# Cross attentions of a two-layer decoder: GpSimd's order of routed rows, norm power and projection bias

## The chip, the cores and the metric

The kernel runs on one core of a Trainium2 chip. The metric is the device time of one execution in microseconds (us), lower is better. Five engines work side by side and meet only at semaphores: TensorE (PE, matrix products; PEld is its weight load), VectorE (DVE), ScalarE (ACT), GpSimd (POOL) and SyncE (SP). DMAs are issued from the queues of SP and POOL and run on the core's 16 DMA engines.

## The reference

Eight sequences of 256 tokens with 256 features go through two layers. In both, a self-attention, a cross-attention to 77 context rows and a mixture of eight experts (the two best are taken for every token) add to the tokens `x`:

```
x = x + _L0_attn_ref(_layernorm(x, axis=-1), ...)
x = x + _L0_xattn_ref(_layernorm(x, axis=-1), ctx_1024, ctx_1024, ...)
x = x + _L0_ffn_ref(_layernorm(x, axis=-1), ...)       # top 2 of 8 experts
x = x + _L1_attn_ref(_layernorm(x, axis=-1), ...)
x = x + _L1_xattn_ref(ctx_1024, ctx_1024, _layernorm(x, axis=-1), ...)
x = x + _L1_ffn_ref(_layernorm(x, axis=-1), ...)       # top 2 of 8 experts
```

A cross-attention's output projection has a bias (`bo`), and the norm that follows it feeds the router of the experts.

## The kernel before

The change lies in `attention_crossed`, which runs once in each layer (names begin with L0x and L1x). It works through B = 8 batches (sequences) of 256 tokens. A batch is two tiles of 128 tokens (QT_N = 2) and is worked on in two units u = 2b + c, one for each half of the heads. The order of the work is written out by hand, once for every engine, as a loop over the units; no scheduler moves anything. Several batches are in flight in one turn of the loop. While the attention of batch b runs:

- the first norm (before the attention) is made for batch b+2: DVE statistics, POOL `spread_norm`, ACT `norm`;
- batch b-1 gets its projection added (DVE `add`, L498) and then its second norm, the one for the router: DVE statistics (L501 to L506), POOL `route_norm` (four small instructions, L255 to L258: add epsilon, the power -1/2, the product with the mean, the sign), ACT `route_norm` (L627, which writes the normed rows `xr`), PE transposes of `xr` (L804) and the router's product (L809);
- batch b-2 gets its two experts chosen (DVE `choose`, L514 to L529), and batch b-3 its slots in the experts' table (DVE `slots`, up to L546);
- `send` (L744) scatters the rows of batch b-3 into the table `expert_table` in device memory: an indirect DMA on POOL's queue for each of the two tiles and each of its two experts, four for a batch, each of 128 rows of 260 floats. Each adds 16 to the semaphore `scattered[b % 2]`.

The rows to be sent stand in `xr[b % 2]`, two buffers. So ACT's `route_norm` of batch b, which overwrites the buffer of batch b-2, has to wait until all of batch b-2's rows have been scattered:

```
eng.wait_ge(r_rstd_done, b + 1)
if b >= 2:
    eng.wait_ge(scattered[par], b // 2 * 64)
```

The bias of the projection is added to X by POOL (`bias`, L725) ahead of DVE's `add` of the same batch, which comes two units later. SP's queue waits for scattered rows at three places: it loads early blocks of the table (L2167) when batches 0 to 3, and then 0 to 4, have been sent, and the rest at the end. POOL's `send` of batch 4, and of batch 5, in turn waits for these early loads to land (`early_landed`), in front of its first tile. Behind the loop POOL sends batch 5, adds to the experts' part, and works on the second norm and the rows of batches 6 and 7.

On PE the order in a unit with c = 0 is: the scores of the next unit, the transposes of maxima, the query projection (L300), the transposes of `xr` (L804), the values of the unit before (L865), the turned scores (L850).

Of the kernel before, what the change touches and what calls it, by code (L numbers as in the profile page):

```python
# [309 lines left out]
def attention_crossed(nc, name, env, wo, bo, first, route, experts, final):  # L310
# [33 lines left out]
    with ExitStack() as stack:  # L344
# [95 lines left out]
        with nc.Block(no_gpsimd_drain=True) as block:  # L440
            @block.sync
            def _(eng):
                for b in range(B):
                    eng.wait_ge(added, b + 1)
                    tiles = slice(b * QT_N, (b + 1) * QT_N)
                    eng.dma_start(route["sums"].rearrange("(t p) d -> p t d", p=P)[:, tiles, :], X[:, tiles, :]).then_inc(route["kept"], 16)
                    if b == ORDER_BY + 1:
                        experts["first_loads"](eng)
                    for i, last in enumerate(FULL_BY):
                        if b == last + 1:  # L450
                            for par in range(2):
                                eng.wait_ge(scattered[par], ((last - par) // 2 + 1) * 64)
                            experts["load_early"](eng, i)
                for sc in scattered:
                    eng.wait_ge(sc, B // 2 * 64)
                experts["sync"](eng)
# [260 lines left out]
            @block.gpsimd  # L717
            def _(eng):
                def route_norm(b):
                    first["spread"](eng, b, r_mv, r_veps, r_rstd, r_offset, r_shift_by, r_var_done, r_rstd_done)  # L720

                def bias(b):
                    xb = X[:, b * QT_N:(b + 1) * QT_N, :]
                    eng.wait_ge(xn_done, b + 1)
                    eng.tensor_tensor(xb, xb, bo[:, :].unsqueeze(1).to_broadcast([P, QT_N, D]), ALU.add).then_inc(biased, 1)  # L725

                def odds_of(b):

                    eng.wait_ge(apart_done, b + 1)
                    eng.wait_ge(slot_done, b)  # L730
                    eng.tensor_tensor(odds[:, :], env["e"][:, 0:QT_N], apart[:, :], ALU.pow).then_inc(odds_done, 1)

                def send(b, tiles=range(QT_N)):
                    par = b % 2
                    eng.wait_ge(slot_done, b + 1)
                    if b == 0:
                        for s, v in route["zeroed"]:
                            eng.wait_ge(s, v)
                    for i, last in enumerate(FULL_BY):
                        if b == last + 1 and tiles[0] == 0:  # L740
                            eng.wait_ge(*experts["early_landed"][i])
                    for q in tiles:
                        for k in range(TOP):
                            eng.indirect_dma_start(route["table"], bass.IndirectOffsetOnAxis(ap=slot_i[:, par, q, k:k + 1], axis=0),  # L744
                                                   xr[:, par, q, :], None).then_inc(scattered[par], 16)

                for i in range(2):
                    eng.memset(tops[i][:, :, :], 0.0).then_inc(cleared, 1)
                first["clear"](eng, 1)
                first["weights_in"](eng)  # L750
                if ("b", 0) in events:
                    eng.wait_ge(first["bias_out"], 1)
                for u in range(units):
                    b, c = part(u)
                    if c == 0:
                        if b + 2 < B:
                            first["spread_norm"](eng, b + 2)
                        if b >= 3:
                            send(b - 3)
                    else:  # L760
                        bias(b)
                        if b >= 1:
                            route_norm(b - 1)
                x = experts["pool_parts"](eng)
                send(B - 3)
                x["start"]()
                odds_of(B - 2)
                route_norm(B - 1)
                x["add"](0)
                send(B - 2, [0])  # L770
                odds_of(B - 1)
                send(B - 2, [1])
                send(B - 1)
                for n in range(1, len(EARLY)):
                    x["add"](n)
                x["rest"]()
# [1968 lines left out]
```

## Time and profile before

| | us |
|---|---|
| median of 3 runs | 1502.38 |
| lowest and highest | 1500.22, 1503.75 |
| the profiled execution, device time | 1504.03 |
| its span in the trace | 1502.4 |
| cross-attention of layer 0 in the trace | about 225 to 385 |
| cross-attention of layer 1 in the trace | about 1078 to 1240 |
| TensorE busy, mean of the span | 95% |

The profiled execution lies 1.65 us over the median, and its span leaves out 1.6 us around the program. A time worked out in the trace is added to 1504.03; against the median it reads 1.65 us less. Both cross-attentions have the same structure, so a row of one layer stands for both unless said otherwise.

### The profile page before, as it was taken

What the parts mean: (1) busy time and instruction counts of PE and PEld (TensorE: products, weight loads), DVE (VectorE), ACT (ScalarE), POOL (GpSimd) and SP (SyncE); (2) the same over time, 40 slices, a digit from 0 to 9 for tenths busy, and PEclk for the clock granted to TensorE, in tenths of its full rate; (3) what the DMA queues carried; (4) which work ended last, traced back from release to release, by engine and by line L of the source; (5) the groups of instructions that cost most, each with busy time, mean ns of one, the idle gap of its engine ahead of it and who ended that gap; (6) DMA issues with size and microseconds to landing.
All of it is one profiled execution on the core that took longest, in us unless ns stands there. A gap on an engine that the chain in (4) does not pass through costs nothing. (4 is left out here: it accounts for less than half of the span.)

```text
span 1502.4 us, 34667 instructions
## 1 busy us (share of the span) xinstructions
PE 1433.9 (95%) x11880; PEld 1159.7 (77%) x11881; DVE 748.7 (50%) x2160; ACT 619.1 (41%) x1711; POOL 490.5 (33%) x758
## 2 busy tenths in 40 slices
PE   7999998988999999999999999999899899999998
PEld 5676766767899999976777777777666579999997
DVE  6666757887433333344444444444278862222222
ACT  2433346653222222235445444545366533333332
POOL 3545442444322122223233233333224452222222
PEclk9999999999999999999999999999999999999999
DMA  9920000152243434120000000000001522533332
GB/s 316 333 69 2 2 2 9 45 176 62 50 119 67 144 71 114 32 64 1 0 1 1 1 1 1 1 1 0 1 16 44 174 78 40 149 93 94 94 90 34
DMA packets 79666, 97.46 MB, mean 65 GB/s; under 512 B 10523, under 2 KB 72579, under 8 KB 79555
## 3 DMA queue, kind: packets, MB, share of 16 engines
q1 hardware_dynamic: 64643, 77.58, 16.4%
q0 software_dynamic: 13680, 17.19, 6.6%
q8 instruction: 73, 1.20, 0.3%
q10 hardware_dynamic: 1232, 1.18, 0.2%
q14 instruction: 38, 0.31, 0.1%
HBM read 57.51 MB, written 39.59 MB: 65 GB/s over the span
## 5 line engine op out<-in xcount | busy, mean ns | idle before, releaser
L1741 POOL TENSOR_TENSOR L1a_prob<-L1a_prob,L1a_rtot 128x1024 f32<-128x1024 f32 x64 | 121.1, 1892 | 275.8 <-DVE L1a_rtot L1614 275.8
L2270 PEld LDWEIGHTS L0x_ps<-L0f_rows_t,L0f_w_up 128*128 128x128 f32 x1584 | 183.7, 193 | 10.4 <-issue 9.0
L2270 PE MATMUL L0x_ps<-L0f_rows_t,L0f_w_up 128*128 128x128 f32 x1584 | 185.8, 277 | 5.6 <-issue 4.8
L2346 ACT ACTIVATE L1f_hid<-L1x_ps,L1f_b_up 128x128 f32<-128x128 f32 x296 | 92.4, 363 | 163.0 <-PE L1x_ps L2270 159.7
L2270 PEld LDWEIGHTS L1x_ps<-L1f_rows_t,L1f_w_up 128*128 128x128 f32 x1184 | 139.5, 194 | 3.4 <-issue 1.6
L2270 PE MATMUL L1x_ps<-L1f_rows_t,L1f_w_up 128*128 128x128 f32 x1184 | 140.4, 277 | 0.6 <-ACT L1f_rows_t L2330 0.6
L2279 PE MATMUL L1x_ps<-L1f_w_down,L1f_hid 128*128 128x256 f32 x592 | 134.1, 380 | 1.9 <-issue 1.9
L2214 POOL TENSOR_TENSOR turn<-eps 128x1 f32<-128x1 f32 x74 | 13.6, 184 | 372.3 <-DVE wv L2448 367.7
L1683 ACT ACTIVATE L1a_prob<-L1a_ps_s,L1a_nmax 128x256 f32<-128x256 f32 x256 | 118.2, 473 | 38.1 <-DVE L1a_nmax L1609 38.1
L2279 PEld LDWEIGHTS L1x_ps<-L1f_w_down,L1f_hid 128*128 128x128 f32 x592 | 109.6, 190 | 15.5 <-issue 2.1
L1245 POOL TENSOR_SCALAR_AFFINE_SELECT L0a_prob<-L0a_prob 128x128 f32<-128x128 f32 (+1 forms) x256 | 79.8, 353 | 104.3 <-ACT L0a_prob L1199 104.3
L2338 ACT ACTIVATE ctx_in<-L0x_ps 128x256 f32<-128x256 f32 x72 | 27.6, 383 | 183.1 <-PE L0x_ps L2270 157.1
L2279 PE MATMUL L0x_ps<-L0f_w_down,L0f_hid 128*128 128x256 f32 x432 | 99.4, 380 | 1.7 <-DVE L0f_hid L2435 1.7
L1199 ACT ACTIVATE L0a_prob<-L0a_ps 128x384 f32<-128x384 f32 x128 | 52.4, 497 | 108.0 <-PE L0a_ps L1331 108.0
L1609 DVE TENSOR_REDUCE L1a_nmax<-L1a_ps_s 128x2 f32<-128x512 f32 x128 | 79.2, 681 | 31.4 <-PE L1a_ps_s L1805 31.4
L2279 PEld LDWEIGHTS L0x_ps<-L0f_w_down,L0f_hid 128*128 128x128 f32 x432 | 79.3, 190 | 11.2 <-DVE L0f_hid L2435 1.9
L1819 PEld LDWEIGHTS L1a_ps_t<-ident,L1a_prob 128*128 128x128 f32 x500 | 59.6, 141 | 34.6 <-issue 26.3
L2435 DVE TENSOR_TENSOR L0f_hid<-ctx_in,L0x_ps 128x256 f32<-128x256 f32 x72 | 30.2, 420 | 106.0 <-ACT ctx_in L2338 70.1
L1819 PE MATMUL L1a_ps_t<-ident,L1a_prob 128*128 128x128 f32 x500 | 76.9, 276 | 3.3 <-DVE L1a_prob_t L1618 2.4
L1618 DVE COPY L1a_prob_t<-L1a_ps_t 128x512 f32<-128x512 f32 x63 | 42.8, 680 | 58.3 <-PE L1a_ps_t L1819 58.3
L1693 ACT ACTIVATE L1a_prob_t<-L1a_ps_t 128x512 f32<-128x512 f32 x62 | 37.1, 598 | 81.5 <-PE L1a_ps_t L1819 81.5
L2425 DVE TENSOR_SCALAR token<-L1f_from_end 128x1 int32<-128x1 f32 x37 | 5.7, 153 | 126.8 <-DMA out_dram<-wv,token 126.8
(486 smaller groups left out, 2812.5 us busy)
## 6 DMA issues: line engine op xcount, KB each, us to landing
expert_table<-zero SPq DMA_DIRECT2D x1, 16640.0 KB, 68.5
L0f_w_up<-in_w_dram SPq DMA_DIRECT2D x8, 1408.0 KB, 6.8
L1f_w_up<-in_w_dram SPq DMA_DIRECT2D x8, 1024.0 KB
L1f_w_down<-in_w_dram SPq DMA_DIRECT2D x8, 1024.0 KB
L0f_w_down<-in_w_dram SPq DMA_DIRECT2D x8, 768.0 KB, 8.7
L1f_rows<-expert_table SPq DMA_DIRECT2D x35, 130.0 KB
L0f_rows<-expert_table SPq DMA_DIRECT2D x32, 130.0 KB
sums<-X SPq DMA_DIRECT2D x8, 256.0 KB
```

Of the source, the lines that this page charges most:

```text
L1199: eng.activation(prob[u % 2][:, r, :, :], bank("p", u, r)[:, 0:KT * W].rearrange("p (t w) -> p t w", t=KT), ACT.Exp).then_inc(exp_done, 1)
L1245: ins = eng.affine_select(out=p, in_=p, compare_op=ALU.is_ge, fill=0.0, base=base, pattern=[[0, 2], [sign, n]], channel_multiplier=-sign)
L1609: eng.tensor_reduce(nmax[:, j % RING, :], src, AX.X, ALU.max, negate=True).then_inc(max_done, 1)
L1618: eng.tensor_copy(prob_t[s % 2][:, k, :], turn_bank(b, s, k)).then_inc(even_out, 1)
L1683: ins = eng.activation(prob[:, j % RING, q, :], ps_s[:, k, q * S:(q + 1) * S], ACT.Exp, bias=nmax[:, j % RING, q:q + 1], accum_out=total[: ...
L1693: eng.activation(prob_t[s % 2][:, k, :], turn_bank(b, s, k), ACT.Copy).then_inc(odd_out, 1)
L1741: eng.tensor_tensor(v, v, r.unsqueeze(2).to_broadcast([P, 2 * QT_N, S]), ALU.mult).then_inc(norm_done, 1)
L1819: ins = eng.transpose(out[:, o:o + P], prob[:, j % RING, q, c * P:(c + 1) * P], ident[:, :])
L2270: ins = eng.matmul(ps_h[c][:, o:o + P], w_up[par][:, t, w0:w0 + P], rows_t[:, t, :], start=(t == 0), stop=(t == DT - 1))
L2279: ins = eng.matmul(ps_y[:, 0:D], hid[:, c, k * P:(k + 1) * P], w_down[par][:, 2 * c + k, :], start=(c == 0 and k == 0), stop=(c == CHUNKS ...
L2346: ins = eng.activation(hid[:, c, k * P:(k + 1) * P], ps_h[c][:, k * P:(k + 1) * P], ACT.Gelu, bias=b_up[par][:, 2 * c + k:2 * c + k + 1])
L2435: ins = eng.tensor_tensor(hid[:, c, :], mid[:, c, :], ps_h[c][:, 2 * P:4 * P], ALU.mult)
```

## The change

POOL's loop over units is reordered. Before, the unit c = 0 issued `spread_norm(b + 2)` and all four scatters of batch b-3, and the unit c = 1 the bias of batch b and then the second norm of batch b-1. Now the unit c = 0 scatters only tile 0 of batch b-3 (two DMAs); the unit c = 1 first does the second norm of batch b-1, then scatters tile 1 of batch b-3 (two DMAs), and adds the bias of batch b last. No instruction is added or taken away, and no other engine's order is touched.

```diff
                         if b >= 3:
-                            send(b - 3)
+                            send(b - 3, [0])
                     else:
-                        bias(b)
                         if b >= 1:
                             route_norm(b - 1)
+                        if b >= 3:
+                            send(b - 3, [1])
+                        bias(b)
```

POOL in the cross-attention of layer 0, batch b = 3, the first with a `send`. Before:

```order
L744 DMA expert_table<-L0x_xr,L0x_slot_i 17024x260 [waits zeroed,L0x_slot_done]
L744 DMA expert_table<-L0x_xr,L0x_slot_i 17024x260 x3
L725 TENSOR_TENSOR X<-X,bo 128x512 [waits L0x_xn]
L255 TENSOR_TENSOR L0x_r_veps<-L0x_r_mv,eps 128x2 [waits L0x_r_var]
L256 TENSOR_TENSOR L0x_r_rstd<-L0x_r_veps,neg_half 128x2 [waits L0x_link_g]
L257 TENSOR_TENSOR L0x_r_offset<-L0x_r_mv,L0x_r_rstd 128x2 [waits L0x_link_g]
L258 TENSOR_SCALAR L0x_r_shift_by<-L0x_r_offset 128x2 [waits L0x_link_g]
L255 TENSOR_TENSOR L0x_veps<-L0x_mv,eps 128x2 [waits L0x_var]
```

and of the change at the same place:

```order
L744 DMA expert_table<-L0x_xr,L0x_slot_i 17024x260 [waits zeroed,L0x_slot_done]
L744 DMA expert_table<-L0x_xr,L0x_slot_i 17024x260
L255 TENSOR_TENSOR L0x_r_veps<-L0x_r_mv,eps 128x2 [waits L0x_r_var]
L256 TENSOR_TENSOR L0x_r_rstd<-L0x_r_veps,neg_half 128x2 [waits L0x_link_g]
L257 TENSOR_TENSOR L0x_r_offset<-L0x_r_mv,L0x_r_rstd 128x2 [waits L0x_link_g]
L258 TENSOR_SCALAR L0x_r_shift_by<-L0x_r_offset 128x2 [waits L0x_link_g]
L744 DMA expert_table<-L0x_xr,L0x_slot_i 17024x260 [waits zeroed,L0x_slot_done]
L744 DMA expert_table<-L0x_xr,L0x_slot_i 17024x260
L725 TENSOR_TENSOR X<-X,bo 128x512 [waits L0x_xn]
L255 TENSOR_TENSOR L0x_veps<-L0x_mv,eps 128x2 [waits L0x_var]
```

Two of the four DMAs and the bias have moved behind the second norm, which itself waits for DVE's statistics (`r_var`).

ACT at the same place, which is the same before and after (the second norm of batch 2, L627, and what follows it):

```order
L660 ACTIVATE L0x_counts<-L0x_ps 128x32 [waits L0x_made]
L627 ACTIVATE L0x_xr<-X,L0x_r_shift_by,L0x_r_rstd 128x256 [waits L0x_scattered0,L0x_r_rstd]
L627 ACTIVATE L0x_xr<-X,L0x_r_shift_by,L0x_r_rstd 128x256
L232 ACTIVATE L0x_q_raw<-L0x_ps,bq1s 128x256 [waits L0x_made]
L232 ACTIVATE L0x_q_raw<-L0x_ps,bq1s 128x256
L236 ACTIVATE L0x_q_m<-L0x_q_raw,L0x_none,half_mask 128x2x256 [waits L0x_q_out]
```

Nothing moved on ACT; `scattered0`, for which L627 waits, is counted up by the four DMAs of batch 0, two of which stand elsewhere on POOL now.

## Rows read from the trace of the kernel before

**Rows 1.** The page: busy us of each engine, share of the span, instructions.

```profile
PE 1433.9 (95%) x11880; PEld 1159.7 (77%) x11881; DVE 748.7 (50%) x2160; ACT 619.1 (41%) x1711; POOL 490.5 (33%) x758
```

**Rows 2.** Busy time by window, five batches, layer 0: length, busy us by engine, clock.

```profile
276.20:292.70 16.50, 15.93 (x178) 11.39 (x171) 13.77 (x37) 11.38 (x26) 6.96 (x10) 1.00 0.14 50
292.70:308.40 15.70, 15.45 (x184) 10.87 (x180) 15.12 (x44) 9.93 (x23) 8.13 (x15) 1.00 0.16 53
308.40:326.20 17.80, 15.43 (x180) 10.82 (x176) 16.33 (x62) 10.09 (x22) 7.68 (x12) 1.00 0.74 262
326.20:342.80 16.60, 13.40 (x172) 9.01 (x168) 13.00 (x41) 7.31 (x17) 6.55 (x9) 1.00 0.31 102
342.80:359.00 16.20, 13.75 (x144) 10.19 (x141) 14.30 (x45) 7.20 (x15) 8.12 (x11) 0.89 0.24 74
```

**Rows 3.** Timeline of POOL, batch 3, layer 0: start, length, instruction, idle before, releaser.

```profile
277.10 1.22 POOL L744 DMA_INDIRECT expert_table<-L0x_xr,L0x_slot_i  x1 [0.66 <-issue]
...
281.18 0.96 POOL L744 DMA_INDIRECT expert_table<-L0x_xr,L0x_slot_i  x1 [0.30 <-issue]
282.17 1.27 POOL L725 TENSOR_TENSOR X<-X,bo 128x512 f32<-128x512 f32 x1
286.68 0.19 POOL L255 TENSOR_TENSOR L0x_r_veps<-L0x_r_mv,eps 128x2 f32<-128x2 f32 x1 [3.24 <-DVE L0x_r_mv L506]
...
288.04 0.22 POOL L258 TENSOR_SCALAR L0x_r_shift_by<-L0x_r_offset 128x2 f32<-128x2 f32 x1
292.74 0.20 POOL L255 TENSOR_TENSOR L0x_veps<-L0x_mv,eps 128x2 f32<-128x2 f32 x1 [4.48 <-DVE L0x_mv L183]
```

**Rows 4.** Timeline of ACT and PE behind POOL's norm, batch 3, layer 0.

```profile
287.36 1.89 PE L300 MATMUL L0x_ps<-L0x_xt,wq 128*128 128x256 f32 x8
...
288.30 1.09 ACT L627 ACTIVATE L0x_xr<-X,L0x_r_shift_by,L0x_r_rstd 128x256 f32<-128x256 f32 x2 [1.79 <-POOL L0x_r_shift_by L258]
...
289.53 0.63 PE L804 MATMUL L0x_ps<-ident,L0x_xr 128*128 128x128 f32 x4 [0.28 <-ACT L0x_xr L627]
```

**Rows 5.** Timeline, batch 6, layer 0: last scatter of batch 3, SP's load behind it.

```profile
330.42 0.96 POOL L744 DMA_INDIRECT expert_table<-L0x_xr,L0x_slot_i  x1 [0.30 <-issue]
...
332.23 1.44 DVE L468 TENSOR_REDUCE L0x_tops<-L0x_ps 128x16 f32<-128x1232 f32 x1 [3.05 <-remote]
...
333.70 0.89 SPq L2167 DMA_DIRECT2D ctx_in<-expert_table  x2
```

**Rows 6.** Timeline, batch 5, layer 1: scatter of batch 2, ACT's wait for it.

```profile
1170.62 0.96 POOL L744 DMA_INDIRECT expert_table<-L1x_xr,L1x_slot_i  x1 [0.30 <-issue]
...
1177.89 1.09 ACT L627 ACTIVATE L1x_xr<-X,L1x_r_shift_by,L1x_r_rstd 128x256 f32<-128x256 f32 x2 [1.14 <-DMA expert_table<-L1x_xr,L1x_slot_i]
```

**Rows 7.** Timeline of PE, layer 1: the projection behind batch 4's second norm.

```profile
1170.66 1.97 PE L797 MATMUL L1x_ps<-wo,L1x_o_t 128*128 128x256 f32 x8 [0.85 <-DVE L1x_o_t L483]
```

**Rows 8.** Timeline of DVE in `choose`, layer 0: batches 3, 4 (with POOL's bias), 7.

```profile
284.12 0.17 DVE L522 CAST L0x_index_f<-L0x_index 128x4 f32<-128x4 uint32 x1
...
298.93 1.78 DVE L522 CAST L0x_index_f<-L0x_index 128x4 f32<-128x4 uint32 x1
...
299.40 1.27 POOL L725 TENSOR_TENSOR X<-X,bo 128x512 f32<-128x512 f32 x1
...
347.65 2.00 DVE L524 TENSOR_TENSOR L0x_chosen<-numbers,L0x_index_f 128x16 f32<-128x16 f32 x2
```

**Rows 9.** Timeline behind the loop, layer 0: second norms of batches 6 and 7.

```profile
356.71 1.09 ACT L627 ACTIVATE L0x_xr<-X,L0x_r_shift_by,L0x_r_rstd 128x256 f32<-128x256 f32 x2 [3.70 <-POOL L0x_r_shift_by L258]
...
360.63 0.60 PE L804 MATMUL L0x_ps<-ident,L0x_xr 128*128 128x128 f32 x4
...
367.14 0.19 POOL L255 TENSOR_TENSOR L0x_r_veps<-L0x_r_mv,eps 128x2 f32<-128x2 f32 x1 [2.07 <-DVE L0x_r_mv L506]
```

**Rows 10.** Busy time by window around the end of layer 0's cross-attention, as rows 2.

```profile
352.00:354.00 2.00, 0.54 (x12) 0.45 (x16) 1.93 (x4) 1.00 (x3) 0.00 (x0) 1.00 0.32 85
...
356.00:358.00 2.00, 2.00 (x12) 2.00 (x11) 1.90 (x7) 1.09 (x2) 1.34 (x4) 0.50 0.04 8
```

## The prediction, made before the change was run

> **What bounds the kernel now.** I read the page first: PE is busy for 95% of the span, POOL for 33% [rows 1]. POOL alone sets nothing, so the change can only act through those who wait for POOL. Then the busy time by window, batch by batch, of layer 0's cross-attention [rows 2]. A batch (two units) takes 15.7 to 17.8 us. In batches 3 and 4 PE is busy for all but 0.6 and 0.3 us, in the later ones for all but 2.4 to 3.2 us; DVE is idle for 2.7, 0.6, 1.5, 3.6 and 1.9 us. So both are near their bound, and a stop of PE that is longer than this idle time has nowhere to hide. Third the timeline of POOL [rows 3]: in batch 3 the four scatters run from 277.10 to 282.14, the bias to 283.44, and then POOL stands idle for 3.24 us until DVE's statistics come; the second norm ends at 288.26. ACT starts its part at 288.30, 0.04 us later [rows 4], and ends at 289.39. PE has just ended the query projection (287.36 + 1.89 = 289.25) and has waited 0.28 us for ACT when its transposes start at 289.53 [rows 4]. So the chain DVE statistics, POOL norm, ACT norm, PE transposes is tight: what delays ACT's L627 delays PE one to one.
>
> **The change, part by part.** The work on POOL stays the same: four scatters, one bias of 1.27 us, four small instructions for each norm. Three things move.
>
> *The bias goes last.* DVE's add needs it two units later, about one batch of 16 us; it now ends some 4 us behind the norm. Between the second norm and the next first norm POOL idled 4.48 us [rows 3], and two scatters and the bias (2.5 + 1.3 us) fit in. I cost it at nothing; without this cover it would be 1.3 us a batch.
>
> It also takes something away. In batch 3 DVE's small conversion L522 takes 0.17 us, in batch 4 1.78 us, and in batch 7 the two L524 together 2.00 us instead of 0.26 [rows 8]. In both slow cases POOL's bias runs at that moment: the 1.78 us end at 300.71, the bias at 300.67 [rows 8]. There are three such places in both layers together (a second CAST of 1.78 us in layer 1), 1.61 + 1.74 + 1.61 = 5.0 us of DVE time at most. With the bias behind the norm they should go. But they lie where PE is the tighter one for most of it, or inside a batch that will now be stopped anyway, so I take 2 us of the 5 as gain (bounds 0 and 5).
>
> *The second norm goes ahead of the bias.* Before, POOL had idled 3.24 us in front of it and waited for DVE each time, so this brings nothing: 0.
>
> *Tile 1's scatters go behind the second norm of batch b-1.* Here the change costs. ACT's L627 of batch b-1 waits for `scattered` of batch b-3, since it overwrites that buffer, and it needs the count of all four DMAs. Two of these are now issued only after POOL has finished the very norm that L627 also waits for. The wait was over by then in nearly all batches; now it always ends last. Its price: 0.2 us to the first issue, 1.06 + 0.30 + 0.96 us for two scatters (the last of the four [rows 3] takes 0.96 us behind 0.30 us of issue; the first one takes 1.22 in batch 3 and 1.06 in the later ones), 2.5 us in sum, and then the landing. For the landing there are two rows. With few other DMAs running, the last scatter of batch 3 ends its issue at 331.38 and SP, which waits for it, issues its load at 333.70 [rows 5]: 2.3 us, an upper bound of the quiet case. While the experts' weights are loaded, the last scatter ends its issue at 1171.58 and ACT, waiting for it, starts at 1177.89 [rows 6]: 6.3 us. So ACT's L627 comes 2.5 + 2.2 = 4.7 us later in a quiet batch, and 2.5 + 6.3 = 8.8 us in batch 5, when those loads run. Behind it on ACT stand the query's outputs, the router's outputs and the exponentials; PE waits at L804, directly behind, with the values (L865) and the turned scores (L850) queued.
>
> Batch by batch, for one layer:
> - b = 3: 4.7, since PE waits for ACT already [rows 4].
> - b = 4: 4.7 less the 0.85 us that PE later waits for DVE [rows 7]: 3.8.
> - b = 5: 8.8 at most. In the next unit DVE now waits 3.05 us for something that the profile only calls remote, right behind the heavy loads [rows 5]; with a stop in front of it I expect that wait to be gone. In layer 0 the loads end sooner behind the scatters. I take 5.0 (bounds 3 and 8.8).
> - b = 6: 4.7.
> - b = 7: ACT's norm of batch 6 ended at 357.80, and PE wants it at 360.63 [rows 9]: 2.8 us of slack, so 4.7 - 2.8 = 1.9.
> - behind the loop: the send of batch 5 waits for the early load, which waits for tile 1 of batch 4. 2.5 us of issue, 2.2 us of landing and a load of 2 to 3 us follow POOL's norm of batch 6 (356.67), so batch 5's four scatters start near 365 instead of 357.17, take 5.1 us, and the norm of batch 7, which waited for DVE until 367.14 [rows 9], starts near 371.5 where the shift by 1.9 alone would give 369. That is about 2.0 for PE (bounds 0 and 3).
>
> Sum of a layer: 4.7 + 3.8 + 5.0 + 4.7 + 1.9 + 2.0 = 22.1 us, for two layers 44.2.
>
> *The clock of TensorE.* At the end of layer 0's cross-attention PE was busy for 0.54 of 2.00 us, and in the window from 356 to 358 the granted clock stood at 0.50 [rows 10], that is 1.2 instead of 2.4 GHz. A stop of 4.7 us is longer, so I expect dips in several of the eight stops of the loop. What of a dip lies in the stop itself costs nothing; 2 us of it behind the stop cost 1 us of work. I take half of that for each stop (bounds 0 and 3), 4 us in all.
>
> Total: 44.2 - 2 + 4 = 46.2. On the profiled execution's 1504.03 this gives 1550.2, against the median 1548.6. I forecast 1550.
>
> **The rivals.**
>
> *A, the clock falls at every stop and stays down.* For it: the dip behind a much shorter gap [rows 10]; against it: only what falls behind the stop costs anything. If each of the eight stops is followed by 3 us lost instead of 0.5, it is 8 x 2.5 = 20 us more: 1570. The Trainium skill's page "TensorE: Matmul & The Clock Gate", Part 1, says that the array's clock goes down to half when PE has been little busy and returns after it has been busy again; by that rule every stop is a candidate, and the trace agrees as far as rows 10 show one.
>
> *B, half of each stop is swallowed.* DVE is the tighter engine in batches 4 and 5 (idle 0.6 and 1.5 us [rows 2]), and while PE stands, DVE can run ahead with statistics and slots. Against it: DVE's next reciprocal needs the values that PE has queued behind L804. If half of the 44 us goes so: 1504 + 22 - 2 = 1524, up to 1530 with dips.
>
> *C, faster.* DVE is the true bound, the stop of 4.7 us falls wholly in time in which PE and ACT would have waited for DVE, and what remains is the 5.0 us of DVE time that the moved bias gives back: 1504 - 5 = 1499. It decides from the point where ACT and PE have 4.7 us of slack at L627. The rows give 0.28 us of wait on the wrong side in batch 3 [rows 4], 0.85 us in batch 4 [rows 7]. The Trainium skill's page "SBUF — State Buffer", section "SBUF: two separate sides", has the rule behind this gain: VectorE and GpSimd share a pair of ports, and an instruction of the one can block the other's for its whole length. The 1.78 us agree with that.
>
> *D, no difference.* The scatters of tile 1 land early enough because POOL comes to them before it waits for `r_var`. The order on POOL excludes it, unless I misread which count L627 waits for: 1504.
>
> **How the numbers follow.** The forecast (1534 to 1566 with its own bounds: 3 to 8.8 for b = 5, 0 to 3 behind the loop, 1 us either way for the landing in each stop) gets 0.72, A 0.12, B 0.10, C 0.03, D 0.03. The range from 1524 to 1572 takes in A and most of B. A measurement of this kernel can tell about 0.2%, 3 us, from no change. So slower has 0.72 + 0.12 + 0.10 = 0.94, the same 0.03, faster 0.03.
>
> **What would show it.** In the profile of the changed kernel: L627 waiting for the DMA of `expert_table` in ten places (batches 2 to 6 of both layers), 4 to 5 us behind POOL's L258, up to 9 us in batch 5; PE idle in front of L804 for the same time; batches of 20 to 22 us in both cross-attentions; L522 back at 0.17 us; the experts and self-attentions unchanged. It would be wrong if L627 still waited for POOL's L258, or if PE's idle time in front of L804 were well under 4 us. Shorter dips or none would take 4 us off; a landing nearer to 1 us than to 2.2 would take off some 10.

## The result, and the profile after

| | before | after |
|---|---|---|
| median of 3 runs, us | 1502.38 | 1568.46 |
| lowest and highest, us | 1500.22, 1503.75 | 1566.29, 1571.29 |
| span of the profiled execution, us | 1502.4 | 1566.8 |
| mean granted clock of TensorE in it | 0.993 | 0.965 |

The change makes the kernel slower: the ratio is 1.0444, 95% interval 1.0418 to 1.047, or 66 us. That lies in the predicted range (1524 to 1572), but 18 us over the forecast of 1550, and close to the 1570 of rival A. One execution behind this document, of the kernel with only the bias moved, took 2110.34 us at a mean clock of 0.651; the ratios leave it out.

First the page of the kernel after, its engines' busy us and shares, to be held against [rows 1]:

```profile
PE 1472.6 (94%) x11880; PEld 1185.8 (76%) x11881; DVE 744.6 (48%) x2160; ACT 618.4 (39%) x1711; POOL 490.9 (31%) x758
```

The instruction counts are the same. PE is busy for 38.7 us more (1472.6 against 1433.9) with exactly the same products, and idle for 25.7 us more (1566.8 - 1472.6 = 94.2 against 1502.4 - 1433.9 = 68.5). These two add up to the 64.4 us by which the span grew. So waiting is the smaller part of the loss; the larger is that PE works more slowly.

Next where it lies, in two windows of each kernel that begin and end at the same events (length, busy us of PE, PEld, DVE, ACT and POOL, clock, DMA share, GB/s): first from the end of layer 0's experts over layer 1's self-attention to the start of its cross-attention, then the experts of layer 0. Before, then after:

```profile
640.60:1078.20 437.60, 428.79 (x2587) 319.99 (x2585) 197.16 (x417) 211.56 (x677) 134.29 (x93) 1.00 0.02 6
396.00:640.60 244.60, 239.01 (x1789) 227.06 (x1788) 82.47 (x334) 52.15 (x153) 53.74 (x62) 1.00 0.36 87
```

```profile
668.20:1105.70 437.50, 428.77 (x2587) 320.32 (x2585) 197.35 (x417) 211.53 (x677) 134.26 (x92) 1.00 0.02 6
423.50:668.20 244.70, 239.04 (x1789) 227.17 (x1788) 82.51 (x334) 52.16 (x153) 53.75 (x62) 1.00 0.36 87
```

Both stretches are unchanged to 0.1 us. All of the loss is in the cross-attentions with their tails (from the clearing of `tops` to the first transposes of the experts' rows): 170.7 to 198.3 us in layer 0, 172.5 to 209.7 in layer 1, or 27.6 and 37.2 us.

Now the view of one line, for ACT's L627: what it waited for, and who waited for it (PE's transposes of `xr` stand at L806 now), us and times. Before it had waited 1.1 us once for a DMA.

```profile
  DMA expert_table<-L1x_xr,L1x_slot_i: 30.0, 5
  DMA expert_table<-L0x_xr,L0x_slot_i: 26.4, 5
...
who waited for it (us, times):
  PE L1x_ps L806: 20.9, 5
  PE L0x_ps L806: 18.0, 6
```

Five waits in each layer, ten in all, as the prediction listed. In the timeline of batch 3, layer 0, the chain of [rows 3, 4] reads now:

```profile
287.26 1.89 PE L300 MATMUL L0x_ps<-L0x_xt,wq 128*128 128x256 f32 x8
...
287.94 0.22 POOL L258 TENSOR_SCALAR L0x_r_shift_by<-L0x_r_offset 128x2 f32<-128x2 f32 x1
...
288.66 1.06 POOL L744 DMA_INDIRECT expert_table<-L0x_xr,L0x_slot_i  x1 [0.50 <-issue]
...
290.02 0.97 POOL L744 DMA_INDIRECT expert_table<-L0x_xr,L0x_slot_i  x1 [0.30 <-issue]
291.02 1.27 POOL L725 TENSOR_TENSOR X<-X,bo 128x512 f32<-128x512 f32 x1
292.56 1.09 ACT L627 ACTIVATE L0x_xr<-X,L0x_r_shift_by,L0x_r_rstd 128x256 f32<-128x256 f32 x2 [6.16 <-DMA expert_table<-L0x_xr,L0x_slot_i]
```

```profile
293.80 0.95 PE L806 MATMUL L0x_ps<-ident,L0x_xr 128*128 128x128 f32 x4 [4.65 <-ACT L0x_xr L627]
```

POOL's norm ends at 288.16, as before. Then come the two scatters, the second of which ends its issue at 290.99; 1.57 us later ACT starts, 4.40 us behind the norm where it had been 0.04. PE has waited 4.65 us in place of 0.28, and its four transposes then take 0.95 us instead of 0.63. The last number leads to the clock. Windows of the kernel after in which the granted clock stands at half (columns as in [rows 2]); four of layer 0, then four of layer 1:

```profile
294.00:297.40 3.40, 3.40 (x25) 2.19 (x26) 1.55 (x6) 3.08 (x7) 0.00 (x0) 0.50 0.00 0
314.50:324.70 10.20, 10.20 (x78) 6.41 (x75) 6.66 (x22) 5.00 (x10) 2.33 (x4) 0.50 0.63 202
338.40:348.60 10.20, 10.20 (x72) 6.75 (x63) 5.04 (x13) 3.56 (x9) 0.36 (x1) 0.50 0.05 15
358.90:365.70 6.80, 6.59 (x53) 3.06 (x53) 2.69 (x8) 0.66 (x2) 1.94 (x2) 0.50 0.37 119
...
1178.10:1191.70 13.60, 13.46 (x89) 9.00 (x90) 7.79 (x27) 6.41 (x13) 3.40 (x6) 0.50 0.06 21
1222.50:1236.10 13.60, 11.97 (x84) 7.72 (x85) 4.39 (x7) 5.68 (x11) 0.22 (x1) 0.50 0.08 30
1246.40:1260.00 13.60, 12.34 (x72) 7.96 (x72) 5.35 (x24) 4.00 (x9) 1.94 (x2) 0.50 0.18 60
1273.70:1283.90 10.20, 9.53 (x37) 8.74 (x38) 1.49 (x13) 3.58 (x12) 5.26 (x7) 0.50 0.36 119
```

The delayed L806 start at 293.80, 313.81, 337.00 and 359.11 in layer 0; the windows begin from 0.2 us ahead of them to 1.4 us behind. In layer 1 they begin 0.1 to 1.7 us ahead of L806, while PE still stands. So in these eight places the clock goes down (from 2.4 to 1.2 GHz) when PE has just gone on or is about to, and the half speed falls almost wholly on the work behind the stop: PE is busy for 88% of such a window or more. Behind the two shortest waits of the ten, those of L806 at 1202.27 (1.83 us) and 382.96 (1.44 us), no such window begins. Over the span, but for one at its very end in both kernels, there are 13 such stretches with 105.8 us, of which PE is busy for 100.9; before there were 3 with 17.1 us, busy for 16.3. That is 100.9 - 16.3 = 84.6 us more of work at half speed. At full speed it would take half as long, so 42 us of it would be stretch, against the 38.7 us that PE is busier.

### The profile page after: what moved, and what is told of

It is laid out like the page before. It is cut to its first block and busy times, and to the rows that moved or that the text cites. A ratio compares the mean times of both kernels' runs of the same rounds, so it can differ in the third digit from the quotient of the medians.

```text
span 1566.8 us, 34669 instructions
## 1 busy us (share of the span) xinstructions
PE 1472.6 (94%) x11880; PEld 1185.8 (76%) x11881; DVE 744.6 (48%) x2160; ACT 618.4 (39%) x1711; POOL 490.9 (31%) x758
## 5 line engine op out<-in xcount | busy, mean ns | idle before, releaser
L2272 PEld LDWEIGHTS L0x_ps<-L0f_rows_t,L0f_w_up 128*128 128x128 f32 x1584 | 185.7, 195 | 10.6 <-issue 9.2
L2272 PE MATMUL L0x_ps<-L0f_rows_t,L0f_w_up 128*128 128x128 f32 x1584 | 188.1, 279 | 5.7 <-issue 4.8
L2272 PEld LDWEIGHTS L1x_ps<-L1f_rows_t,L1f_w_up 128*128 128x128 f32 x1184 | 140.8, 195 | 3.4 <-issue 1.6
L2272 PE MATMUL L1x_ps<-L1f_rows_t,L1f_w_up 128*128 128x128 f32 x1184 | 141.7, 279 | 0.6 <-ACT L1f_rows_t L2332 0.6
L2216 POOL TENSOR_TENSOR turn<-eps 128x1 f32<-128x1 f32 x74 | 13.6, 184 | 374.4 <-DVE wv L2450 370.7
L1110 DVE TENSOR_REDUCE L0a_tops<-L0a_ps 128x2 f32<-128x384 f32 x128 | 62.5, 552 | 12.1 <-PE L0a_ps L1316 12.1
```

Of the source, the lines that this page charges most:

```text
L1110: eng.tensor_reduce(tops[u % UNITS][:, :, at_row], src, AX.X, ALU.max, negate=True).then_inc(max_done, 1)
L2272: ins = eng.matmul(ps_h[c][:, o:o + P], w_up[par][:, t, w0:w0 + P], rows_t[:, t, :], start=(t == 0), stop=(t == DT - 1))
```

## The experiments

The median of the kernel before was 1500.1 to 1500.5 us in all of these; ratios are against it. The change itself was timed beside 1502.38, so differences between its 1568.46 and the medians below can be off by some 2 us. The theory at the outset: the loss is the late landing of tile 1's rows, which ACT waits for in ten places, with PE stopping directly behind it, and some part of it is TensorE's clock. Rivals: the moved bias; the scatters being issued in two parts; a loss by stops alone.

### Which of the moved steps costs

The bias alone goes last, all four scatters stay ahead of the norm:

```diff
                             send(b - 3)
                     else:
-                        bias(b)
                         if b >= 1:
                             route_norm(b - 1)
+                        bias(b)
```

> Only the bias moves: all four scatters stay in the unit c = 0, the second norm comes next, the bias last. Theory (the loss is ACT's L627 waiting for tile 1's scatters): nothing of the loss is here, and the three places where DVE's L522 or L524 took 1.6 to 1.7 us longer beside the bias go: 1497 to 1502 us, no L627 waiting for the DMA beyond the 1.1 us of the kernel before. Rival (the late bias delays DVE's add or the next first norm): over 1510, with DVE's L498 waiting for POOL.

Measured: 1500.33 us, ratio 0.9993 (0.9982 to 1.0004). Tile 1's scatters alone go behind the norm, the bias stays where it was:

```diff
-                            send(b - 3)
+                            send(b - 3, [0])
                     else:
                         bias(b)
                         if b >= 1:
                             route_norm(b - 1)
+                        if b >= 3:
+                            send(b - 3, [1])
```

> Only tile 1's scatters move behind the second norm; the bias stays ahead of the norm. Theory: the whole loss of 66 us is here, 1560 to 1572 us, with L627 waiting for the DMA in ten places, 4.1 to 5 us behind L258 and about 8 us once in layer 1. Rival (half of the loss is the bias's): 1530 to 1545.

Measured: 1567.33 us, ratio 1.045 (1.0428 to 1.0472). And the scatters in two parts, but tile 1's ahead of the norm, with the bias last:

```diff
-                            send(b - 3)
+                            send(b - 3, [0])
                     else:
-                        bias(b)
+                        if b >= 3:
+                            send(b - 3, [1])
                         if b >= 1:
                             route_norm(b - 1)
+                        bias(b)
```

> The scatters are split as in the change, but tile 1's stand ahead of the second norm: unit c = 1 is scatter, norm, bias. Theory (what costs is that the scatter is queued behind a norm that waits for DVE, not the split): POOL issues tile 1 directly behind tile 0, so 1497 to 1503 us. Rival (the split or its additional waits cost by themselves): over 1510.

Measured: 1500.14 us, ratio 0.9995 (0.9985 to 1.0006). So the whole loss belongs to one thing, the place of tile 1's scatters behind the norm. Cutting the send in two costs nothing, and moving the bias neither costs nor gains in these kernels. In the kernel with only the bias moved, the view of the line L522 (duration in ns: min, median, max) shows that the conversions of 1.78 us [rows 8] are gone:

```profile
L522 DVE CAST L0x_index_f<-L0x_index x8: 170/170/421, 265.6 to 373.6; 128x4 f32<-128x4 uint32 x8
L522 DVE CAST L1x_index_f<-L1x_index x8: 170/170/415, 1122.9 to 1225.8; 128x4 f32<-128x4 uint32 x8
```

The time that DVE got back did not reach the end.

### The wait for the buffer

A third pair of buffers for `xr` and `slot_i` in layer 0, on top of the change: L627 of batch b then waits for the rows of batch b-3, sent a batch ago. Layer 1 stays as in the change.

```diff
-        xr, xr_t = sb("xr", [P, 2, QT_N, ROW]), sb("xr_t", [P, DT, S])
+        XB = 2 if final else 3
+        xr, xr_t = sb("xr", [P, XB, QT_N, ROW]), sb("xr_t", [P, DT, S])
...
-                    if b >= 2:
-                        eng.wait_ge(scattered[par], b // 2 * 64)
+                    if b >= XB:
+                        eng.wait_ge(scattered[b % XB], b // XB * 64)
```

> The changed order in full, but in layer 0 alone the routed rows and their slots have three buffers, so ACT's L627 waits for the scatters of three batches earlier; layer 1 keeps two. Theory: layer 0 loses nothing any more in the loop and little behind it (the sends of batch 5 still wait for the early load), its share of about half of the 66 us goes: 1532 to 1542 us, L0x_xr with no wait for the DMA, no TensorE clock dips in layer 0's loop, and layer 1 as in the changed kernel. Rival (the late scatters themselves, through SP's loads or the DMA queue, cost): layer 0 keeps over 10 us of its loss, over 1545.

Measured: 1544.8 us, ratio 1.0294 (1.0274 to 1.0315). The line L628 (L627 with one line more ahead of it): what it waited for, and who waited for it (PE's transposes of `xr` stand at L807):

```profile
  DMA expert_table<-L1x_xr,L1x_slot_i: 28.9, 5
...
  PE L1x_ps L807: 20.4, 6
  PE L0x_ps L807: 5.2, 3
```

The wait for the DMA is gone in layer 0 and is there in layer 1. Layer 0's stage takes 176.0 us (170.7 before, 198.3 in the change), layer 1's 207.7 (209.7 in the change). POOL's order is that of the change in both. So what costs is the wait for the buffer, not the order on POOL as such: 22.3 of layer 0's 27.6 us go with it. What remains, 5.3 us, is in the tail, where batch 5 is still sent late: at batch 6's transposes this kernel stands at 360.66 and the kernel before at 360.63, at batch 7's it stands at 373.93 against 369.99, with PE waiting for the late norm:

```profile
373.93 0.63 PE L807 MATMUL L0x_ps<-ident,L0x_xr 128*128 128x128 f32 x4 [4.11 <-ACT L0x_xr L628]
```

My expectation left that too small, which is why it was missed by 3 us. It also missed on the clock: one half-clock stretch of 3.4 us stands inside layer 0's loop (from 344.4), where the change had four. A third buffer in the kernel before was not run; there L627 had waited for the DMA only once, 1.1 us in layer 1.

### One and four scatters behind the norm

Three scatters ahead of the norm and one behind it, and in the second kernel none ahead and four behind:

```diff
-                            send(b - 3, [0])
+                            send(b - 3, [0], [(0, 0), (0, 1), (1, 0)])
...
-                            send(b - 3, [1])
+                            send(b - 3, [1], [(1, 1)])
```

> Dose, downward: of batch b-3's four scatters three stay ahead of the second norm and only the last one stands behind it. Theory (each stop is the issue behind the norm plus the landing of about 1.6 us): L627 comes 2.9 to 3.2 us behind L258 instead of 4.1 to 4.5, so 1.27 us less in ten places, and fewer or shorter half-clock stretches: 1540 to 1556 us. Rival (a fixed price as soon as any scatter is behind the norm): 1562 to 1570 us.

```diff
-                        if b >= 3:
-                            send(b - 3, [0])
                     else:
...
-                            send(b - 3, [1])
+                            send(b - 3)
```

> Dose, upward: all four scatters stand behind the second norm. Theory: two more issues of 1.27 us in ten places, L627 6.6 to 7.0 us behind L258, 25 us for the stops and up to 15 for the clock: 1590 to 1612 us. Rival (fixed price): 1562 to 1572 us.

Measured: 1553.43 us, ratio 1.0342 (1.0317 to 1.0368), with one; 1596.7 us, ratio 1.0628 (1.0604 to 1.0652), with four. Batch 3 of layer 0 in their timelines, one scatter late, then four:

```profile
286.98 0.23 POOL L258 TENSOR_SCALAR L0x_r_shift_by<-L0x_r_offset 128x2 f32<-128x2 f32 x1
...
290.31 1.09 ACT L627 ACTIVATE L0x_xr<-X,L0x_r_shift_by,L0x_r_rstd 128x256 f32<-128x256 f32 x2 [4.87 <-DMA expert_table<-L0x_xr,L0x_slot_i]
```

```profile
288.31 0.22 POOL L258 TENSOR_SCALAR L0x_r_shift_by<-L0x_r_offset 128x2 f32<-128x2 f32 x1
...
295.91 1.09 ACT L627 ACTIVATE L0x_xr<-X,L0x_r_shift_by,L0x_r_rstd 128x256 f32<-128x256 f32 x2 [9.12 <-DMA expert_table<-L0x_xr,L0x_slot_i]
```

ACT comes 3.10, 4.40 and 7.38 us behind the norm with one, two and four late scatters: 1.3 to 1.5 us for each (the issue of 0.96 to 1.22 us and the 0.30 us between two of them), and a landing that is nearly the same in all (1.56, 1.57 and 1.68 us from the end of the last issue to ACT's start). The whole time follows with 53, 66 and 96 us. But already one scatter costs 53 of the 66 us. PE's waits in front of the transposes come to 30.7, 38.9 and 54.9 us in both layers, and PE is busier than before by 35.1, 38.7 and 51.7 us. So in these profiled executions the first late scatter brings 35.1 us of stretched work, the second 3.6, the other two 13.0. The steps are rough: the four executions with one late scatter lie between 1550.27 and 1557.34 us, and the profiled one is the longest.

### The clock

To tell the clock from the waiting, PE gets something to do in the stops: idle products (the identity matrix times itself, results not read) in the eight places of the loop, b = 3 to 6 in each layer, ahead of PE's wait for `xr`. First 30 of them a place, in the change and in the kernel before; then 16.

```diff
+                        if 2 <= t[1] <= B - 3:
+                            idle_products(eng, out, ident, 30)
```

> The changed kernel, with 30 products of the identity that nobody reads (0.12 us each, 3.7 us in all) on TensorE ahead of its wait for xr in batches 2 to 5 of both layers. They lie in the stop, and keep TensorE busy there. Theory (of the 66 us about 39 are the stops of TensorE and the rest, some 25, is the half clock behind them): no half-clock stretches behind these stops, 2 to 6 us lost where a stop was shorter than the products, 1542 to 1555 us. Rival (the clock costs little since DVE is as near to its bound, and the stops are all): 1566 to 1575 us.

> The kernel before with the same 30 products in the same eight places: a stop of 3.7 us for the chain on TensorE, without idle time and with no scatter moved. Theory (what delays TensorE at this point delays the batch nearly one to one, at full clock): 8 x 3.7 = 29 us less some slack, 1522 to 1530 us. Rival B of the prediction (half of each stop is swallowed): 1510 to 1517 us.

Measured: 1551.56 us, ratio 1.0345 (1.0323 to 1.0367), in the change; 1544.9 us, ratio 1.0295 (1.0277 to 1.0313), in the kernel before. The timeline of PE in the change with 30 products, where the stop of batch 3 was:

```profile
286.43 1.89 PE L300 MATMUL L0x_ps<-L0x_xt,wq 128*128 128x256 f32 x8
288.16 6.86 PE L44 MATMUL L0x_ps<-ident 128*128 128x128 f32 x60
294.86 0.60 PE L808 MATMUL L0x_ps<-ident,L0x_xr 128*128 128x128 f32 x4
```

A product takes 0.229 us (6.86 / 30; it stands as two records), about twice what I had sized it at. So the expectation for the kernel before was missed: the products were 54.9 us of added work, not half of that. The 1542 to 1555 for the change held, but by luck, since it was worked out from the same 3.7 us a place. The products last longer than the stops. Still the change with them is 17 us faster than the change without: its mean clock is 0.993 again, and the half-clock stretches add up to those of before (17.1 us). Against the kernel before with the same products, the change costs 6.7 us in place of 66.

With 16 products (3.73 us a place in the records, 29.8 us in all) most stops are no longer covered:

> The change with 16 idle products on TensorE instead of 30, in the same eight places ahead of its wait for the moved batch's rows; their results are not read. At the 0.229 us that one such product took they last 3.66 us a place, which is less than most of the stops. If the dips of TensorE's clock behind the stops carry some 20 us of the loss, the half-clock stretches of the change (105.8 us in all) mostly go, and the time is 1535 to 1546 us, below that with 30 products (1551.6). If the products with 30 had won their time in another way, the half-clock time stays near 100 us and the time is 1562 or more.

> The kernel before with the same 16 products in the same eight places: 8 x 3.66 = 29.3 us more work on TensorE, results not read. With 30 products 81 per cent of the added work reached the end; if that holds, the time is 1520 to 1527 us. If the stretch behind each place swallows a fixed amount of some 2 to 3 us, so that short stops are mostly taken back, it is below 1515 us.

Measured: 1541.68 us, ratio 1.026 (1.0232 to 1.0288), in the change; 1516.98 us, ratio 1.0097 (1.007 to 1.0123), in the kernel before. Batch 3 in the timeline of PE of the change with 16 products (its transposes of `xr` stand at L808):

```profile
288.18 3.73 PE L44 MATMUL L0x_ps<-ident 128*128 128x128 f32 x32
292.89 0.66 PE L808 MATMUL L0x_ps<-ident,L0x_xr 128*128 128x128 f32 x4 [0.98 <-ACT L0x_xr L627]
```

and windows of the same kernel over the loop of layer 0, where the clock had been down four times in the change (they end where this kernel's first half-clock stretch begins, behind the last of the products):

```profile
286.00:302.00 16.00, 14.77 (x144) 12.12 (x141) 11.27 (x31) 8.01 (x17) 7.85 (x12) 1.00 0.12 41
302.00:322.00 20.00, 19.75 (x221) 15.24 (x223) 17.39 (x64) 10.48 (x23) 8.04 (x13) 1.00 0.40 129
322.00:346.00 24.00, 21.70 (x260) 15.81 (x252) 15.17 (x48) 11.09 (x25) 7.69 (x12) 1.00 0.41 148
346.00:363.80 17.80, 15.59 (x183) 11.44 (x185) 12.75 (x38) 8.00 (x17) 5.48 (x6) 1.00 0.19 61
```

The stops still hold PE's transposes up: products and waits in front of them come to 29.8 + 14.4 = 44.2 us, 5 more than the 38.9 us of waits in the change. Yet the kernel with 29.8 us of useless work is 26.8 us faster than the change. With half-clock stretches of 37.5 us in place of 105.8, PE's own products take 1470.3 - 29.8 = 1440.5 us in place of 1472.6. PE is busy at half clock for 36.0 us in place of 100.9, and half of the difference is 32.4. This is the clock, shown: 32.1 us less of stretched work, 5.4 us more of products and idle time (99.6 against 94.2), together the 26.7 us of the spans.

The kernel before with the products answers a second question: what is a hold-up of PE worth by itself, at full clock? 29.8 us of it cost 16.9 (1516.98 - 1500.1), 54.9 us cost 44.6 (1544.9 - 1500.3). From the one to the other every us comes through (27.7 for 25.1); 10 to 13 us do not, 1.3 to 1.6 a place. The 1516.98 us missed both readings of the expectation: 81% of the added work coming through (1520 to 1527 us; it was 57%), and 2 to 3 us swallowed at each place (below 1515). What fits the two kernels is the second with a smaller amount.

### The tail

For the last batch of the loop, b = 7, all four scatters go ahead of the norm again; the rest is the change:

```diff
-                            send(b - 3, [0])
+                            send(b - 3, [0] if b < B - 1 else [0, 1])
...
-                        if b >= 3:
+                        if 3 <= b < B - 1:
```

> The change, but for the last batch (b=7) all four sends go ahead of the norm, as before. My theory: the tail term (1.9 us on ScalarE for batch 6 and 2.0 us behind the loop, 3.9 a layer) and the half-clock stretches that these two stops bring go, and the time is 1552 to 1562 us. If the tail's delay is made up again in the experts, or comes from batch 5 alone, it stays at 1566 to 1570 us.

Measured: 1554.16 us, ratio 1.0351 (1.0325 to 1.0376), so 14.3 us less than the change; the profiled executions differ by 17.6. Layer 0's stage is 3.7 us shorter (198.3 to 194.6), about the 3.9 us of the forecast. Layer 1's is 13.8 us shorter, and not all of that is the tail: its batch 5 hit a shorter landing. The same place in the timelines, of the change and then of this kernel:

```profile
1216.35 0.96 POOL L744 DMA_INDIRECT expert_table<-L1x_xr,L1x_slot_i  x1 [0.30 <-issue]
...
1222.73 1.09 ACT L627 ACTIVATE L1x_xr<-X,L1x_r_shift_by,L1x_r_rstd 128x256 f32<-128x256 f32 x2 [7.61 <-DMA expert_table<-L1x_xr,L1x_slot_i]
```

```profile
1212.32 0.96 POOL L744 DMA_INDIRECT expert_table<-L1x_xr,L1x_slot_i  x1 [0.30 <-issue]
...
1215.49 1.09 ACT L627 ACTIVATE L1x_xr<-X,L1x_r_shift_by,L1x_r_rstd 128x256 f32<-128x256 f32 x2 [4.07 <-DMA expert_table<-L1x_xr,L1x_slot_i]
```

In the change ACT starts 5.42 us behind the end of the issue, while the experts' weights are loaded: the DMA engines move 374 GB/s in these 5.4 us. In this kernel it starts 2.2 us behind, with 145 GB/s moving, and PE waits 2.49 us in place of 6.18. Nothing in the edit aims at that. The stage begins 4 us earlier in this kernel, and the scatters fall differently against the loads. That the time lies in the expected 1552 to 1562 us is therefore in part luck. How much of layer 1's 13.8 us is the tail and how much this stays open.

All in one table, from the pages (PE's busy time without the added products, and its idle time, both against the kernel before; us). The sum of the two and of the added products is the growth of the profiled span, which may differ from that of the medians by some us:

| kernel | median | added products | PE busier | PE more idle |
|---|---|---|---|---|
| the change | 1568.46 | 0 | +38.7 | +25.7 |
| one scatter late | 1553.43 | 0 | +35.1 | +18.2 |
| four late | 1596.7 | 0 | +51.7 | +42.4 |
| third buffer in layer 0 | 1544.8 | 0 | +23.1 | +17.0 |
| b = 7 as before | 1554.16 | 0 | +33.8 | +13.0 |
| the change, 16 products | 1541.68 | 29.8 | +6.6 | +1.3 |
| the change, 30 products | 1551.56 | 54.9 | -4.2 | -4.7 |
| before, 16 products | 1516.98 | 29.8 | -5.2 | -11.8 |
| before, 30 products | 1544.9 | 54.9 | -4.1 | -12.1 |

In the last three rows PE's own work comes out 4 to 5 us below the kernel before, two of them with its 17.1 us of half-clock stretches, so a few us of this column may lie in how overlapping records are added up.

No kernel that was run beats the kernel before; the two that equal it (1500.33 and 1500.14 us) leave tile 1's scatters ahead of the norm.

## Why the prediction was right, and where its sum was not

The sign, the place and the mechanism hold: ten waits of L627 for the DMA of `expert_table`, in batches 2 to 6 of both layers, PE stopped behind it, the rest of the kernel unchanged. The range held the time, in part by luck. The sum was built from two kinds of terms, and both were off, in opposite directions. The forecast had 44 us of waiting and 4 of clock; the page after has 25.7 us of waiting and 38.7 of slower work. The 1534 to 1566 called the forecast's own bounds did not hold it: these used neither the bounds of the clock (0 to 3 us a stop) nor those of the bias (0 to 5), and the range reached to 1572 for rival A.

**The stops one by one.** Predicted was L627 4.7 us behind the norm, up to 8.8 in batch 5. Measured: 4.40, 4.16, 5.26, 4.18, 4.28 us in layer 0 and 4.53, 4.08, 7.94, 4.89, 4.34 in layer 1. The landing was 1.6 us in a quiet batch and 5.4 in layer 1's batch 5, both under the upper bounds of [rows 5, 6] (2.3 and 6.3) from which I took them. PE's waits, layer 0 and layer 1: b = 3 4.65 and 4.77 (forecast 4.7); b = 4 2.18 and 1.83 (3.8); b = 5 3.02 and 6.18 (5.0); b = 6 4.10 and 4.81 (4.7); b = 7 1.44 and 3.27 (1.9); behind the loop 2.65 and nothing at this place (2.0). They add up to 38.9 us, against 3.0 before: 36 us more, where I had 44. The prediction named as a sign of being wrong that PE waits well under 4 us in front of these transposes. Five of the ten waits in the loop are 1.4 to 3.3 us, so "what delays ACT's L627 delays PE one to one" held for b = 3 and not in general. The largest misses are b = 4 and b = 6. In b = 6 PE had waited 1.17 us at this place before, which was not taken off. In b = 4 I took off 0.85 us as PE's slack [rows 7]. Before, PE had none there; it ended L300 as ACT ended its norm (304.70 + 1.09 = 305.79):

```profile
304.05 1.89 PE L300 MATMUL L0x_ps<-L0x_xt,wq 128*128 128x256 f32 x8
305.94 0.63 PE L804 MATMUL L0x_ps<-ident,L0x_xr 128*128 128x128 f32 x4
```

and of the change:

```profile
309.73 1.89 PE L300 MATMUL L0x_ps<-L0x_xt,wq 128*128 128x256 f32 x8
313.81 0.63 PE L806 MATMUL L0x_ps<-ident,L0x_xr 128*128 128x128 f32 x4 [2.18 <-ACT L0x_xr L627]
```

From the transposes of batch 3's turn to the end of this L300, PE took 311.62 - 293.80 = 17.8 us in place of 16.4, with the half clock from 294.0 to 297.4 in it. DVE's statistics (L506) ended 12.95 us behind the same start in place of 13.49, with L522 back at 0.17 us. These 1.4 and 0.5 us are what the 4.1 us of delay lost on the way to 2.2 us of wait: the clock's price at one stop is paid in part out of the wait at the next.

**What a stop costs.** PE's idle time grew by 25.7 us though the waits at L806 grew by 36. So about 10 us of other idle time vanished. That is about what the kernels before with products take back, 1.3 to 1.6 us a place; in the change slower work that fills idle time may have a share in it, and the runs do not separate the two. I charged every stop in full: rows 2 had shown 0.6 and 0.3 us of idle time of PE in batches 3 and 4, but 2.4 to 3.2 in the later ones. The step "a stop of PE that is longer than this idle time has nowhere to hide" should have been followed by a subtraction. Rival B had the direction of this right, but not the size (22 us). It also misread [rows 2]: in batch 4 PE was idle for 0.3 us and DVE for 0.6, so DVE was the tighter engine in batch 5 alone. And its reason, DVE running ahead, does not hold for the stop of batch 3, where DVE stood still itself until PE had gone on:

```profile
295.81 0.78 DVE L192 TENSOR_SCALAR L0x_k_s<-L0x_ps,half_mask,L0x_k_bias 128x154 f32<-128x154 f32 x2 [5.27 <-PE L0x_ps L282]
```

**The clock.** This is the term of the sum that was mis-sized. I took 0.5 us a stop, bounds 0 and 3, from "2 us of it behind the stop cost 1 us of work", and from one window of [rows 10]. Measured: half-clock stretches of 3.4 to 13.6 us, almost wholly on PE's work behind the stop (the eight windows above), and 38.7 us of stretched work, 3.9 for each of the ten stops or 4.8 for the eight of the loop, above the upper bound that I set. What [rows 10] could have told me is that the half clock had outlasted the idle time by whole microseconds: PE had been busy for 0.54 us from 352 to 354, and it was busy for 2.00 of 2.00 us at 0.50 in the window from 356 to 358. I read these rows as showing that a dip exists and did not read its length. Rival A, which had 24 us for the clock, was nearer than the forecast; what kept the time from going over its 1570 is what the stops gave back. The Trainium skill's page "TensorE: Matmul & The Clock Gate", Part 1, section "HAM oscillation — how this bites in real kernels", puts the price of stretches at half clock at half of their length, each time PE waits anew for data; the trace agrees, with 42 us by that rule for the 84.6 us of products and the 38.7 us by which PE is busier.

**The bias.** The forecast took 2 us of gain, bounds 0 and 5. The long conversions went, as predicted, and the gain was 0 (0.9993, 0.9982 to 1.0004). The lower bound was right. In batch 4 of layer 0 DVE was not what ended last: PE was still busy with L300 (to 305.94) when ACT's norm was ready at 305.79. The Trainium skill's page "SBUF — State Buffer", section "SBUF: two separate sides", says that VectorE and GpSimd lock one another out of a shared pair of ports. The trace agrees, since the durations of 1.78 us went with the bias; it does not follow that taking such a lock away is worth anything.

**The tail.** 3.9 us a layer were forecast for b = 7 and what lies behind the loop. Putting b = 7 back is worth 3.7 us in layer 0; in layer 1 PE did not wait behind the loop at all. In the kernel with three buffers, too, 5.3 us of layer 0's loss remain, with PE waiting behind the late sends of batch 5. In the change their cause was the one predicted: batch 5's scatters start at 385.83 behind the early load, and the norm of batch 7 follows them directly at 391.97 without a wait of its own, where it had waited for DVE [rows 9].

Rivals C and D fell: the time is not at 1499 or 1504.

The account of the change is thus: stops of 36 us at PE, of which 26 remain as idle time, and 39 us of work stretched by the clock, with 64 us the growth of the span. That the clock's part goes when the stops are filled was shown (kernels with 16 and 30 products). Open is what sets the length of a stretch at half clock (one late scatter already brings 35 us of stretched work, four bring 52), and how layer 1's batch 5 falls against the weight loads: the landing there was 5.4 us in the change and 2.2 with an earlier start of the stage.

## What to carry to other kernels

When a change makes a busy TensorE stop for a few microseconds, cost the stop itself less what is idle nearby anyway, and then the work behind it at half speed for as long as the profile has shown such a stretch to last. Read the length of a dip in the clock's column, not only that it is there. And before work is moved on an engine with idle time, look at who waits for its completion, not its issue: here two DMAs of one microsecond each, moved behind an instruction on an engine busy for a third of the time, cost 4.4%.

## What the runs showed of the hardware

- A shorter stop need not save much of the clock's part. In one profiled execution each, with one scatter late the stops in front of the transposes add up to 30.7 us and PE's work is stretched by 35.1; with two, 38.9 and 38.7; with four, 54.9 and 51.7. For one scatter late the profiled execution was the longest of four (1557.34 us, median 1553.43).
- Work that nobody needs can pay. 16 useless products in each of eight places made the changed kernel 26.8 us faster (1568.46 to 1541.68). The same products made the kernel before, where these waits come to 3.0 us in all, 16.9 us slower.
- An indirect scatter of 128 rows of 260 floats took 0.95 to 1.22 us of POOL (median 0.97), 0.30 us to the next, and landed 1.6 us behind the end of its issue in quiet stretches, 5.4 us while weights were loaded. From issue to landing, min, median and max over the changed kernel:

```profile
DMA to landing us min/median/max: 2.4/2.6/6.6
```

The Trainium skill's page "DMA: Bandwidth & Descriptors", section "Anatomy of one DMA — SWDGE (gpsimd) path", has 2.0 us and the bytes at 436 GB/s, which for 133 kB makes an estimate of 2.3 us; the trace's 2.4 to 2.6 us agree with it, its 6.6 does not.
